# A qkv and output product over 192 features, split as 128 and a doubled 64 in place of 96 and 96

## What is computed

```python
h = patches @ W_lin.T + b_lin                      # and the class token in front
qkv = layernorm(h) @ qkv_weight.T                  # 192 -> 3 x 192
q, k = layernorm(q) * 16 ** -0.5, layernorm(k)     # over the 16 numbers of a head
h = h + (softmax(q @ k.T) @ v) @ proj_weight.T     # per head, then 192 -> 192
h = h + ffn(layernorm(h))                          # experts, 2 of 8, and the shared one
```

## Time and profile before

| | |
|---|---|
| median of three runs | 2127.14 us |
| the profiled execution | 2126.83 us |
| its span, first to last instruction | 2124.9 us |
| TensorE busy, matmuls | 1922.6 us, 90%, 17848 of them |
| VectorE busy | 1320.9 us, 62%, 3554 |
| ScalarE busy | 908.2 us, 43%, 1878 |
| first matmul | at 28.75 us |
| last residual of the attention, L710 | at 1184.90 us |
| mean granted TensorE clock | 0.984 |

### The profile page before, as it was taken

The page is one execution under the profiler, slowest core; times in us unless marked ns, Lnnn a source line. Parts: engine busy times, 40 slices in busy tenths (PEclk is TensorE's granted clock), DMA queues, the critical chain, the costliest instruction groups (busy, mean ns, idle before and its releaser), DMA issues. The chain is left out here.

```text
span 2124.9 us, 48134 instructions
## 1 busy us (share of the span) xinstructions
PE 1922.6 (90%) x17848; PEld 1351.2 (64%) x17848; DVE 1320.9 (62%) x3554; ACT 908.2 (43%) x1878; POOL 42.2 (2%) x63
## 2 busy tenths in 40 slices
PE   3999989899899898998998699999999999999998
PEld 3777767677677776776776355555555555555556
DVE  3444444444344444444444488788888888888888
ACT  2555545455455555555555233333333333333332
POOL 0000000000000000000000000000000000000000
PEclk9999999999999999999999799999999999999999
DMA  4011111111111111111110000000000000000000
GB/s 146 16 45 44 48 43 45 46 44 45 46 45 44 46 44 46 45 45 46 44 44 10 32 16 30 17 21 23 15 30 15 22 22 15 30 15 30 16 21 13
DMA packets 31517, 74.83 MB, mean 35 GB/s; under 512 B 3435, under 2 KB 16366, under 8 KB 31214
## 3 DMA queue, kind: packets, MB, share of 16 engines
q1 hardware_dynamic: 31310, 72.10, 10.8%
HBM read 52.73 MB, written 19.37 MB: 34 GB/s over the span
## 5 line engine op out<-in xcount | busy, mean ns | idle before, releaser
L571 ACT ACTIVATE prob<-ps_sc 99x792 f32<-99x792 f32 x384 | 317.5, 827 | 256.0 <-PE ps_sc L413 256.0
L357 PE MATMUL ps_hid<-lin_f,xin 128*99 128x192 f32 x1536 | 289.9, 333 | 65.7 <-DVE v L684 36.1
L905 PE MATMUL ps_h<-yT_hi,w_hi 96*128 96x512 f16 (+1 forms) x900 | 342.8, 381 | 0.0
L907 PE MATMUL ps_h<-yT_lo,w_hi 96*128 96x512 f16 (+1 forms) x900 | 341.3, 379 | 0.0
L908 PE MATMUL ps_h<-yT_hi,w_lo 96*128 96x512 f16 (+1 forms) x900 | 340.9, 379 | 0.0
L357 PEld LDWEIGHTS ps_hid<-lin_f,xin 128*99 128x99 f32 x1536 | 240.3, 169 | 77.0 <-issue 47.2
L979 ACT ACTIVATE in_hi<-inner 128x512 f16<-128x512 f32 (+1 forms) x225 | 140.3, 624 | 338.3 <-DVE inner L1098 338.3
L923 PE MATMUL ps_y<-w_hi,in_hi 128*128 128x192 f16 (+1 forms) x900 | 222.4, 247 | 40.6 <-DVE acc L1122 29.0
L971 ACT ACTIVATE act<-ps_h 128x512 f32<-128x512 f32 (+1 forms) x225 | 132.3, 588 | 278.6 <-PE ps_h L908 277.9
L1122 DVE SCALAR_TENSOR_TENSOR acc<-ps_y,comb,acc 128x192 f32<-128x192 f32 (+1 forms) x700 | 242.3, 407 | 0.0
L1098 DVE SCALAR_TENSOR_TENSOR inner<-ps_h,act 128x512 f32<-128x512 f32 (+1 forms) x225 | 152.7, 679 | 130.0 <-ACT act L971 119.8
(11 more groups left out here) (112 smaller groups left out, 3050.1 us busy)
## 6 DMA issues: line engine op xcount, KB each, us to landing
xin<-xp SPq DMA_DIRECT2D x64, 594.0 KB, 3.9
hidden_dram<-h SPq DMA_DIRECT2D x64, 147.0 KB
hin<-hidden_dram SPq DMA_DIRECT2D x24, 384.0 KB, 3.0
out<-acc SPq DMA_DIRECT2D x24, 384.0 KB, 2.3
w_f<-w SPq DMA_DIRECT2D x1, 1728.0 KB, 11.5
hidden_dram<-h SPq DMA_DIRECT2D x64, 0.8 KB
w_f<-w SPq DMA_DIRECT2D x1, 864.0 KB, 13.0
lin_f<-w_lin SPq DMA_DIRECT2D x1, 576.0 KB
```

Of the source, the lines that this page charges most:

```text
L357: last = pe.matmul(hid[:, t, :], xin[q][:, k, t * TR:(t + 1) * TR], lin_f[:, k, :], start=(k == 0), stop=(k == PCHUNKS - 1))
L571: act.activation(prob[quad][:, places].rearrange("p h m s -> p h (m s)"), ps_sc[0:TR, places, 0:2 * SLOTS], ACT.Exp, scale=D ** -0.5 / (SQ ...
L905: pe.matmul(bank[:, 0:N], w13_hi[:, k, e, w, :], yT_hi[p][:, k, 0:N], start=(k == 0), stop=False)
L907: pe.matmul(bank[:, 0:N], w13_hi[:, k, e, w, :], yT_lo[p][:, k, 0:N], start=False, stop=False)
```

## The change

The weights of qkv and of the output product are laid out over 128 rows: chunk 0 holds features 0 to 127, chunk 1 features 128 to 191 twice, one copy under the other. Of chunk 1, `hi` becomes [w_hi; w_lo] and `lo` becomes [w_hi; 0] (new operations in the first block). xnorm and o_norm get 256 columns, the last 64 of them a second copy of features 128 to 191, so that the transposes (now 99 x 128) put x on both halves. Then hi x hi of chunk 1 gives x_hi w_hi + x_hi w_lo in one product, and lo x lo gives x_lo w_hi: five products instead of six. The second copies are written by additional VectorE passes over 64 columns, in `norm_hidden` and in `o_out`. In `run` of `phase_a`, `first` goes from 1 to 2.

```diff
-            qkv_hi, qkv_lo = split_pair("qkv", [KC, 2, 3 * C])
-            proj_hi, proj_lo = split_pair("proj", [KC, 2, C])
+            qkv_hi, qkv_lo = split_pair("qkv", [128, 2, 3 * C])
+            proj_hi, proj_lo = split_pair("proj", [128, 2, C])
...
-            xnorm = sb("xnorm", [TR, 2, C])
-            xT_hi = sb("xT_hi", [KC, 2, SLOTS], F16)
-            xT_lo = sb("xT_lo", [KC, 2, SLOTS], F16)
+            xnorm = sb("xnorm", [TR, 2, 256])
+            xT_hi = sb("xT_hi", [128, 2, SLOTS], F16)
+            xT_lo = sb("xT_lo", [128, 2, SLOTS], F16)
...
                     for n, (f, hi, lo, _) in enumerate(weights):
                         dve.wait_ge(w_hi_done, n + 1)
-                        dve.scalar_tensor_tensor(out=lo[:], in0=f[:], scalar=SW, in1=hi[:],
-                                                 op0=ALU.mult, op1=ALU.subtract).then_inc(w_lo_done, 1)
+                        if f in tailed:
+
+                            dve.scalar_tensor_tensor(out=lo[:, 0], in0=f[:, 0], scalar=SW, in1=hi[:, 0],
+                                                     op0=ALU.mult, op1=ALU.subtract)
+                            dve.tensor_copy(lo[0:64, 1], hi[0:64, 1])
+                            dve.memset(lo[64:128, 1], 0.0)
+                            dve.scalar_tensor_tensor(out=hi[64:128, 1], in0=f[64:128, 1], scalar=SW,
+                                                     in1=hi[64:128, 1], op0=ALU.mult,
+                                                     op1=ALU.subtract).then_inc(w_lo_done, 1)
+                        else:
+                            dve.scalar_tensor_tensor(out=lo[:], in0=f[:], scalar=SW, in1=hi[:],
+                                                     op0=ALU.mult, op1=ALU.subtract).then_inc(w_lo_done, 1)
...
         def run(fori, step):
 
-            first = 1
+            first = 2
             for k in range(first * UNROLL):
                 step(Index(0, k))
             with fori(first, IMAGES // UNROLL) as i:
...
-            def products(outs, lhs, rhs, chunks):
-
-                (lhs_hi, lhs_lo), (rhs_hi, rhs_lo) = lhs, rhs
-                for k in range(chunks):
-                    pe.matmul(outs, lhs_hi(k), rhs_hi(k), start=(k == 0), stop=False)
-                    pe.matmul(outs, lhs_hi(k), rhs_lo(k), start=False, stop=False)
-                    last = pe.matmul(outs, lhs_lo(k), rhs_hi(k), start=False, stop=(k == chunks - 1))
-                return last
+            def products(outs, lhs_hi, lhs_lo, rhs_hi, rhs_lo):
+
+                pe.matmul(outs, lhs_hi[:, 0], rhs_hi[:, 0], start=True, stop=False)
+                pe.matmul(outs, lhs_hi[:, 0], rhs_lo[:, 0], start=False, stop=False)
+                pe.matmul(outs, lhs_lo[:, 0], rhs_hi[:, 0], start=False, stop=False)
+                pe.matmul(outs, lhs_hi[:, 1], rhs_hi[:, 1], start=False, stop=False)
+                return pe.matmul(outs, lhs_lo[:, 1], rhs_lo[:, 1], start=False, stop=True)
...
-                        last = pe.transpose(feat[:, k, t * TR:(t + 1) * TR], src[:, t, k * KC:(k + 1) * KC],
+                        last = pe.transpose(feat[:, k, t * TR:(t + 1) * TR], src[:, t, k * 128:(k + 1) * 128],
                                             id32[0:TR, 0:TR])
...
                 for t in range(2):
-                    last = dve.tensor_scalar(xnorm[:, t, :], h[n.mod(HB)][:, t, :], meanvar[:, t, 0:1],
+                    dve.tensor_scalar(xnorm[:, t, 0:C], h[n.mod(HB)][:, t, :], meanvar[:, t, 0:1],
+                                      h_rstd[:, t:t + 1], ALU.subtract, ALU.mult)
+                    last = dve.tensor_scalar(xnorm[:, t, C:256], h[n.mod(HB)][:, t, 128:C], meanvar[:, t, 0:1],
                                              h_rstd[:, t:t + 1], ALU.subtract, ALU.mult)
                 last.then_inc(xnorm_done, 1)
...
-                dve.tensor_tensor(o_norm[:, t, :].rearrange("p (h d) -> p h d", d=D), o_tok[:, :, 0:D],
-                                  o_rden[:, t, :].unsqueeze(2).broadcast_to([TR, HEADS, D]),
-                                  ALU.mult).then_inc(onorm_done, 1)
+                for first, heads in ((0, HEADS), (C, HEADS - 8)):
+                    last = dve.tensor_tensor(
+                        o_norm[:, t, first:first + heads * D].rearrange("p (h d) -> p h d", d=D),
+                        o_tok[:, HEADS - heads:HEADS, 0:D],
+                        o_rden[:, t, HEADS - heads:HEADS].unsqueeze(2).broadcast_to([TR, heads, D]), ALU.mult)
+                last.then_inc(onorm_done, 1)
...
+    def tailed(w):
+
+        w = np.asarray(w).T
+        return np.ascontiguousarray(np.stack([w[0:128], np.concatenate([w[128:C], w[128:C]])], 1))
```

More of the change, by code:

```diff
@@ L136, in vit_layer @@
             lin_f = stage("lin_f", [128, PCHUNKS, C])
-            qkv_f = stage("qkv_f", [KC, 2, 3 * C])
-            proj_f = stage("proj_f", [KC, 2, C])
+            qkv_f = stage("qkv_f", [128, 2, 3 * C])
+            proj_f = stage("proj_f", [128, 2, C])
             gate_f = stage("gate_f", [KC, 2, EXPERTS])
@@ L141, in vit_layer @@
             w2_f = stage("w2_f", [INTER, NE, C])
-            qk_mean = stage("qk_mean", [KC, 2, 2 * HEADS])
+            qk_mean = stage("qk_mean", [128, 2, 2 * HEADS])
             weights = [(qkv_f, qkv_hi, qkv_lo, w_qkv),
@@ L145, in vit_layer @@
                        (w13_f, w13_hi, w13_lo, w13), (w2_f, w2_hi, w2_lo, w2)]
+            tailed = [qkv_f, proj_f]
             others = [(lin_f, w_lin), (id32, ident), (biascls, bias_cls), (gbias, gate_bias), (bef4, before4), (bef8, before8)]
@@ L168, in vit_layer @@
             o_rden = sb("o_rden", [TR, 2, HEADS])
-            o_norm = sb("o_norm", [TR, 2, C])
-            onT_hi = sb("onT_hi", [KC, 2, SLOTS], F16)
-            onT_lo = sb("onT_lo", [KC, 2, SLOTS], F16)
+            o_norm = sb("o_norm", [TR, 2, 256])
+            onT_hi = sb("onT_hi", [128, 2, SLOTS], F16)
+            onT_lo = sb("onT_lo", [128, 2, SLOTS], F16)
             h2 = [sb(f"h2{p}", [TR, 2, C]) for p in range(2)]
@@ L211, in _ @@
                         qk = qkv_f[:, k, 0:2 * C].rearrange("p (h d) -> p h d", d=D)
-                        mean = qk_mean[:, k, :].unsqueeze(2).broadcast_to([KC, 2 * HEADS, D])
+                        mean = qk_mean[:, k, :].unsqueeze(2).broadcast_to([128, 2 * HEADS, D])
                         last = dve.tensor_tensor(qk, qk, mean, ALU.subtract)
@@ L262, in phase_a @@
         hid = ps_hid[0:TR, 0:2 * C].rearrange("p (t c) -> p t c", t=2)
-        x_feat = ps_qk[0:KC, 0:2 * SLOTS].rearrange("p (k s) -> p k s", k=2)
+        x_feat = ps_qk[:, 0:2 * SLOTS].rearrange("p (k s) -> p k s", k=2)
         qk_ps = ps_qk[0:TR, 0:2 * C].rearrange("p (h d) -> p h d", d=D)
         qkT_ps = ps_mix[:, 0:QUADS * TR].rearrange("p (b s) -> p b s", s=TR)
-        o_feat = ps_mix[0:KC, 0:2 * SLOTS].rearrange("p (k s) -> p k s", k=2)
+        o_feat = ps_mix[:, 0:2 * SLOTS].rearrange("p (k s) -> p k s", k=2)
         o_tok = ps_mix[0:TR, 0:QUADS * 128].rearrange("p (h e) -> p h e", e=VB)
@@ L370, in from_xT @@
                 s = slice(t * TR, (t + 1) * TR)
-                return products(outs, (lambda k: xT_hi[:, k, s], lambda k: xT_lo[:, k, s]),
-                                (lambda k: qkv_hi[:, k, cols], lambda k: qkv_lo[:, k, cols]), 2)
+                return products(outs, xT_hi[:, :, s], xT_lo[:, :, s], qkv_hi[:, :, cols], qkv_lo[:, :, cols])
             def qk(n, t):
@@ L451, in project @@
                     s = slice(t * TR, (t + 1) * TR)
-                    last = products(tok[:, t, :], (lambda k: onT_hi[:, k, s], lambda k: onT_lo[:, k, s]),
-                                    (lambda k: proj_hi[:, k, :], lambda k: proj_lo[:, k, :]), 2)
+                    last = products(tok[:, t, :], onT_hi[:, :, s], onT_lo[:, :, s], proj_hi, proj_lo)
                 last.then_inc(proj_done, 1)
@@ L1223 @@
         "xp": xp, "w_lin": chunked(L0_tok_W_lin, 128), "bias_cls": bias_cls,
-        "w_qkv": chunked(L0_attn_qkv_weight, KC), "w_proj": chunked(L0_attn_proj_weight, KC),
+        "w_qkv": tailed(L0_attn_qkv_weight), "w_proj": tailed(L0_attn_proj_weight),
         "w_gate": chunked(L0_ffn_gate_weight, KC), "gate_bias": gate_bias,
```

## The result

The changed kernel takes 2139.2 us, median of five runs (2135.6 to 2142.7), against 2127.1 us before in the same runs: a ratio of 1.006, 95% interval 1.0043 to 1.0077. It is slower by 0.6%, 0.2 us outside the stated range of 2118 to 2139 us, and by 12.1 us, 3.7 times the 3.3 us of the forecast. The profiled execution took 2139.2 us, 12.4 more than before.

A forecast was written before the change was run, and what follows sets the result against it. The attention step was taken as bound by a ring: a ScalarE/VectorE stretch, then a TensorE stretch. 60 x (0.454 - 0.327) = +7.6, jump -4.4, start +0.85, drain -0.7: +3.3 us, so 2130.4 us; range 2118 to 2139.

The forecast's parts named there:

- The ring of two arcs: Attention step: scores to L443 is paced by ScalarE and VectorE (5.60 us), L443 to scores' end by TensorE (11.77 us).
- which products count: Attention step: only savings in qk(n2, 0) and values count, 0.327 us; qk(n2, 1) and project only lengthen the stall before L443.
- The narrow pass: norm_hidden: each added 64-column xnorm pass costs 0.227 us, two cost 0.454 us on each of 60 steps.
- The reading with two columns per cycle: xnorm's added 64-column pass: more time is fixed, 59 ns per tensor-read scalar; 0.227 us a pass, the reading taken.
- the one with one column per cycle: Rival on xnorm's added 64-column passes: 0.161 us a pass, total -4.5 us, 2122.6 us; chance 0.18.
- o_norm's pass and the wider operands: o_out's extra 64-column pass, with 0.24 us of cover, and products over 128 rows: nothing added for either.
- The start: Loading before the attention: 192 KB more weights cost 0.85 us, ends nothing and 1.3; the split's extra VectorE operations are hidden.
- come out even, within 1 us: First attention steps, with the pipeline still filling: no net cost or gain, within 1 us.
- The peeled steps: Attention loop: 16 steps written out instead of 8, five jumps back instead of six; one saved, 4.4 us, ends 2.9 to 6.5.
- The second phase: Feed-forward part after the attention: not touched by the change, so no term in the sum.
- the chain of xnorm costs more: Rival on norm_hidden: a 64-column pass keeps the wide one's 0.294 us; total +11.4 us, 2138.5 us; chance 0.13.
- the longer straight part brings nothing: Rival on the attention loop: written-out code stalls elsewhere or slow stretches take the gain back; +7.7 us, 2134.8 us; chance 0.14.

The follow-up runs named there:

- the passes moved: Changed kernel with norm_hidden split: token block 0 behind qk_variance(n2, 1), token block 1 behind the residual, no instruction added; 2102.9 us, ratio 0.990.
- the four kernels without jumps: All 69 attention steps written out, VectorE's list padded: five products 2103.3 us, six 2095.0; with norm_hidden moved and square earlier, six 2074.3, five 2045.0.

## Why the prediction was wrong, point by point

- *The ring of two arcs, and which products count*: right, and shown by the passes taken out, the passes moved and the four kernels without jumps. A step went from 17.37 to 17.51 us (17.49 forecast as a mean, and 17.49 is the mean over a turn), the stall before L452 from 0.55 to 1.33 (1.3 forecast), that before L367 fell from 0.58 to 0.34, where I had written 0.58: TensorE's transposes of qk_norm come late behind the new o_norm pass, as the prediction says, and eat into it. Embed itself starts 2.20 us after L452, as forecast.
- *The narrow pass*: 0.227 us forecast, 308 ns long and 0.22 us to the next one measured. The reading with two columns per cycle and a price for each scalar read from a tensor gave 309 ns; the one with one column per cycle gave 243. The mode table of the Trainium skill (VectorE: DVE Perf Modes, the perf-mode tier table) agrees with these rows. The 58 cycles of its section on the TRN2 errata give an estimated 94 and 160 ns, where passes here follow each other in 220 and 294; for the duration of a single operation that section itself calls 58 too low and gives about 150 cycles as measured.
- *o_norm's pass and the wider operands*: nothing, as taken. A 192-column product over 128 rows takes 0.25 us, four transposes to 128 columns 0.50 as before.
- *The start*: the first matmul came 0.9 us later (29.63 against 28.75), the number that was forecast for the larger load; but it lies between 28.7 and 29.6 us in the five profiles with six products and between 28.6 and 30.6 in those with five (but for the one with a pad ahead of it), so the agreement shows little. From the first matmul to the first residual the first steps cost 1.9 us more (62.8 against 60.9), where I had "come out even, within 1 us". This is the narrow passes, which lie bare with few images in the pipeline: without them, or with xnorm moved, the stretch takes 60.8 and 60.7 us, when half of the 3.4 us at the low clock in each of the two is taken off.
- *The peeled steps*: this is the step that failed. "One is saved: 4.4 us" took a jump's price as a property of the kernel, with 3 us of allowance for slow stretches. In the changed kernel's profile the remaining five took 7.1 us each, so that the jumps cost 8.4 us more instead of 4.4 less. Of the difference of 12.8 us, 8.5 are the clock: behind five jumps it stood at 1.2 GHz for 34 us, where five of the former price had 17, and half of such time is lost. The other four are longer gaps, 17.6 us where five of the former had 13.7. Even on the kernel before peeling alone saved 2.5 us of jumps in its one profile, and not 4.4. In every profile with the changed kernel's products and a loop a jump costs more (5.9 to 7.2 us in the mean) than in the kernel before and its peeled version (4.5 and 4.9), but the kernel before with xnorm moved has 6.1, so it isn't the five products alone.
- *The second phase*: the prediction said it was not touched. Its code isn't, but its place is, and by place alone VectorE's jumps there have between 0 and 43 us of gaps. The changed kernel happens to lie where they cost nothing, as the kernel before does; with first = 1 it would have lost 34 us of time. The 5.6 us that the profiled execution gained there are mostly less time at the low clock, as shown under the result. Without this chance the profiled pair would differ by some 17 us.

By time the rival "the chain of xnorm costs more" came nearest (2138.5), but its reason is refuted: the pass takes 0.22 us and not 0.294. By reason it is "the longer straight part brings nothing" (2134.8, chance 0.14), whose second ground was that slow stretches take the gain back; they took more than the gain. The sum had the sign right: without any jump the change costs 8.3 us, against the 3.3 forecast with one jump saved and 7.7 without that.

What stays open: what decides how long TensorE's clock stays low behind a jump. Within one profile of the kernel before, jumps with gaps of 2.57 and 2.58 us cost 6.0 and 2.8, so the gap's length alone doesn't; and between the kernel before and the same with xnorm moved the mean went from 4.5 to 6.1 with no instruction added.

## What to carry to other kernels

Walk the ring of waits before counting saved instructions: 0.65 us of TensorE's work per image were saved, half of it in a stretch where VectorE's chain set the pace, and the helper passes that the saving needed were put on exactly that chain; put into gaps where VectorE waited anyway, the same change gains 1.4%. And a kernel with loops must be compared with its loops in the same places: an edit in one phase can cost or give some ten microseconds in a later one (here 34 us), so look in the waits for gaps of issue at the jumps first, and pad or write out before judging an edit. Compare, too, how long the clock stood low in each stretch: stretches that no edit had touched differed by up to 10 us through it.

## What the runs showed of the hardware

The place of VectorE's second loop in its list (307 instructions a turn, eight jumps back) and its gaps of issue in the second phase; the place is counted in the compiled list:

| kernel | loop starts at | beyond a multiple of 256 | gaps, us |
|---|---|---|---|
| before | 894 | 126 | 0.4 |
| before, first = 2 | 1141 | 117 | 0 |
| changed | 1243 | 219 | 0 |
| changed, first = 1 | 964 | 196 | 43.4 |
| the same, padded by 23 | 987 | 219 | 0 |
| changed without narrow passes | 1195 | 171 | 25.1 |
| changed, written out | 2592 | 32 | 25.0 |
| the same, padded by 94 | 2686 | 126 | 0.2 |

That the place decides is shown by the two padded pairs. The rule isn't: 196 is dear and 219 is not. The Trainium skill (Runtime: NRT & Kernel Launch, Instruction fetch mechanics) says that instructions come in blocks of 256, two of which are held, and that a jump to a block that isn't held waits for its load; the gaps agree with that in kind, but a turn of 307 instructions spans two blocks from 196 and three from 219, so by these counts the dear ones are not those that span more blocks. Nor would other borders help: the cheap 219 lies between the dear 196 and 32, the cheap 117 and 126 between 32 and 171, so no shift of the borders parts them. What else decides stays open.

A step costs 0.15 us more inside a loop than written out, in both kernels (17.37 against 17.215, 17.51 against 17.36), with the same instructions of work. In the loop the semaphores are compared with values held in registers; whether that is the reason wasn't tried.
